# Perceiver block on one core: tile 1's attention moved ahead of tile 0's FFN, Wo split between other work, four buffers for x

## The reference

```python
def fake_quant(x, s, z):
    return (clip(round(x / s + z), 0, 255) - z) * s

x = x + fake_quant(layernorm(x), s1, z1) @ fake_quant(ctx, s2, z2)       # per sequence
qkv = layernorm(x) @ Wqkv          # 32 heads of 32 for q, one head for k and v
p = softmax(causal(q k^T / sqrt(32) + alibi))
x = x + (p v) @ Wo
r = softmax(layernorm(x) @ gate_w.T)                                      # 8 experts
x = x + ((layernorm(x) * (r @ in_scale)) @ sign(weight).T) * (r @ out_scale) + bias
```

## Time and profile before

| | us |
|---|---|
| median of 3 runs | 455.34 |
| lowest, highest | 454.68, 456.38 |
| the profiled execution's own time | 456.7 |
| its span, first to last instruction | 454.9 |
| granted TensorE clock, mean | 0.935 |

### The profile page before, as it was taken

One profiled execution on the slowest core, in us unless ns is written; L12 is line 12 of the kernel. 1 busy time (PEld: TensorE's weight loads), 2 busy tenths in 40 slices (PEclk: granted clock), 3 DMA queues, 4 the chain that ended last, 5 costly groups with the idle time before them and its releaser, 6 DMA issues.

```text
span 454.9 us, 9598 instructions
## 1 busy us (share of the span) xinstructions
PE 382.6 (84%) x3952; PEld 260.4 (57%) x3952; DVE 313.5 (69%) x584; ACT 258.9 (57%) x308; POOL 99.7 (22%) x112
## 2 busy tenths in 40 slices
PE   0446965996699998999899989998999899889665
PEld 0115844964245874587458845884588458745332
DVE  7688576875737859785978597859885965384331
ACT  4687986564875757565756575657665622242110
POOL 4420010004112312231223122312131212021202
PEclk9999975799599999999999999999999999989759
DMA  7999993599876964596459745974491010001001
GB/s 316 378 410 409 406 408 128 186 343 414 242 276 226 324 215 140 170 339 213 138 164 337 220 140 165 330 226 138 156 339 43 0 48 1 4 0 48 0 0 46
DMA packets 30049, 91.97 MB, mean 202 GB/s; under 512 B 8208, under 2 KB 8208, under 8 KB 29968
## 3 DMA queue, kind: packets, MB, share of 16 engines
q1 hardware_dynamic: 27840, 83.40, 51.5%
q10 hardware_dynamic: 2160, 7.87, 4.6%
HBM read 85.50 MB, written 4.19 MB: 197 GB/s over the span
## 4 chain that ended last, share of the span: by engine, by line
PE 68%; DMA 11%; DVE 10%; ACT 5%; issue 4%; SPq 1%; POOL 1%; POOLq 0%; DVEq 0%; ACTq 0%
DMA ring<-ctx 11%; PE R L1408 11%; PE T L1245 8%; PE R L1198 7%; PE R L1200 7%; PE R L1199 7%; PE R L1278 6%; PE R L1280 6%; PE R L1281 6%; PE C L1226 5%; ACT b L475 4%; PE T L1367 4%; DVE Pr L913 2%; DVE XL L1012 1%; PE R L1302 1%
## 5 line engine op out<-in xcount | busy, mean ns | idle before, releaser
L475 ACT ACTIVATE b<-ring,quant,qpar 128x2048 uint8<-128x2048 f32 x64 | 132.9, 2091 | 11.6 <-DMA ring<-ctx 11.5
L1278 PE MATMUL R<-T_hi,Wqkv_hi 128*128 128x128 f16 x512 | 90.9, 223 | 0.0
L1280 PE MATMUL R<-T_lo,Wqkv_hi 128*128 128x128 f16 x512 | 90.8, 223 | 0.0
L1281 PE MATMUL R<-T_hi,Wqkv_lo 128*128 128x128 f16 x512 | 90.7, 223 | 0.0
L1278 PEld LDWEIGHTS R<-T_hi,Wqkv_hi 128*128 128x128 f16 x512 | 51.8, 101 | 0.4
L1408 PE MATMUL R<-sgn,T_hi 128*128 128x512 fp8e4 x128 | 51.7, 404 | 0.0
L1408 PE MATMUL R<-sgn,T_lo 128*128 128x512 fp8e4 x128 | 51.6, 403 | 0.0
L1280 PEld LDWEIGHTS R<-T_lo,Wqkv_hi 128*128 128x128 f16 x512 | 51.2, 100 | 0.2
L1281 PEld LDWEIGHTS R<-T_hi,Wqkv_lo 128*128 128x128 f16 x512 | 51.2, 100 | 0.0
L1226 PE MATMUL C<-b,aT 128*64 128x512 f16 x256 | 39.6, 439 | 13.5 <-ACT b L475 11.3
L1198 PE MATMUL R<-Wo,attT_hi 128*128 128x512 f16 x128 | 48.6, 380 | 0.4 <-DVE attT_lo L944 0.4
(11 more groups left out here) (131 smaller groups left out, 821.8 us busy)
## 6 DMA issues: line engine op xcount, KB each, us to landing
ring<-ctx SPq DMA_DIRECT2D x64, 1024.0 KB, 5.9
ring<-L_attn_Wo SPq DMA_DIRECT2D x4, 1024.0 KB, 7.5
ring<-L_ffn_weight SPq DMA_DIRECT2D x4, 1024.0 KB, 5.7
out<-X ACTq DMA_DIRECT2D x8, 512.0 KB, 2.6
Wo<-L_attn_Wqkv SPq DMA_DIRECT2D x7, 544.0 KB, 15.5
XN<-x ACTq DMA_DIRECT2D x6, 512.0 KB, 3.4
sgn<-L_attn_Wqkv SPq DMA_DIRECT2D x1, 544.0 KB, 17.5
X<-x ACTq DMA_DIRECT2D x1, 512.0 KB, 3.8
```

Source lines behind the costliest of these rows:

```text
L475: e.activation(b8[:, c % BRING, :], ring[:, slot, :], ACT.Identity, scale=qR2, bias=qZ2).then_inc(s_rf[slot], 1)
L1278: e.matmul(dst, hi, rows[0], start=k == 0 and g == 0, stop=False, skip_group_check=True)
L1280: e.matmul(dst, hi, rows[1], start=False, stop=False, skip_group_check=True)
L1281: last = e.matmul(dst, lo, rows[0], start=False, stop=k == KT - 1, skip_group_check=True)
```

## The change

Steps 1 and 2 are woven into one list, `step_1(s, ahead)`, with `ahead = Step(2)`. It issues tile 1's PT, PV, `ta` and projection before tile 0's FFN; tile 0's T2 and router lie between; all of context 2 and the `t1` of tile 2 follow, and then `second_half(2)` goes on at `kv`. Tile 1's queries go to C instead of R2, R3, and tile 0's projection to C too (`project_to`, `query_to`). The T turns are a table (`turns`). The FFN reads its own copies XS, so T16 is free earlier, and there are two vbd pairs. `wo_lo` takes one piece at a time between other work of DVE, `wo_hi` likewise on ACT. `norm0(2)` stands behind tile 1's attention rows and waits for four Ta (both tiles'). SP puts `turn_over(2)` ahead of pieces 4 to 7 of context 2. The scales are loaded behind Wqkv and split on DVE in step 1, with fewer operations. X, XN and X2 become four rotating buffers, summed in place; a load waits for the store of the tile that had the buffer.

```diff
@@ SP
                 if s.is_step(2):
-                    load_context(2, 4, 2)
                     turn_over(2)
-                    load_context(2, 6, 2)
-                else:
-                    load_context(s.i, 4, 4)
-                    if s.i > 2:
-                        turn_over(s.i)
+                load_context(s.i, 4, 4)
+                if s.i > 2:
+                    turn_over(s.i)
                 if s.is_step(0):
                     for k in range(KT):
                         e.dma_start(wqkv_raw[k], wqkv_v[:, k, :]).then_inc(s_lw[k], 16)
+                    e.dma_start(small_sb[:, :], small_in).then_inc(s_const, 16)
+                    for k in range(2):
+                        e.dma_start(scales_raw[k], scales_in[:, k, :]).then_inc(s_scales, 16)
@@ helpers
+        def project_to(m, n):
+            return C[:, 1 - n, :] if m == 0 else R[:, n, :]
+        def query_to(i, n):
+            return C[:, n, :] if i == 1 else R[:, 2 + n, :]
@@ DVE norm0
                 if t > 1:
-                    e.wait_ge(s_Ta, (t - 1) * 2)
+                    e.wait_ge(s_Ta, max((t - 1) * 2, 4))
+                if t == 3:
+                    e.wait_ge(s_T1, 6)
@@ DVE scales
             def scales_by_part():
+                e.wait_ge(s_const, 16)
+                e.wait_ge(s_scales, 32)
+                for k in range(2):
+                    part, raw = scales[:, k, :], scales_raw[k]
+                    link(e.tensor_copy(part, raw))
+                    link(e.tensor_scalar(part, part, sign_sb, None, ALU.mult))
+                    last = e.scalar_tensor_tensor(part, raw, lower_sb, part, ALU.mult, ALU.add)
...
@@ ACT, second part of the new list
+            def step_1(s, ahead):
...
+                wo_hi(3)
+                sign(0)
                 ta_hi(s, 0)
+                q_hi(s, 1)
+                k_hi(s)
+                sign(1)
+                ta_hi(s, 1)
+                q_hi(s, 0)
+                sign(2)
+                sign(3)
+                exp(ahead, 0, 0)
+                exp(ahead, 0, 1)
+                conv(2, 0)
+                pt_hi(ahead, 0, 0)
+                pt_hi(ahead, 0, 1)
+                exp(ahead, 1, 0)
+                exp(ahead, 1, 1)
+                conv(2, 1)
+                pt_hi(ahead, 1, 0)
+                pt_hi(ahead, 1, 1)
+                ta_hi(ahead, 0)
+                t2_copy(s, 0)
+                t2_copy(s, 1)
+                conv(2, 2)
+                router_exp(s)
+                ta_hi(ahead, 1)
+                rt_copy(s)
+                conv(2, 3)
+                xs_hi(s, 0)
+                xs_hi(s, 1)
+                for c in range(4, 8):
+                    conv(2, c)
+                outscale_copy(ahead)
@@ DVE
+            def step_1(s, ahead):
+                softmax_rest(0)
+                scales_by_part()
+                x1(s)
+                pt_lo(s, 0, 0)
+                norm1(s)
+                pt_lo(s, 0, 1)
+                wo_lo(0)
+                t1_lo(s, 0)
+                t1_lo(s, 1)
+                wo_lo(1)
+                attn_rows(s, 0, 0)
+                attn_rows(s, 0, 1)
+                v_lo(s)
+                pt_lo(s, 1, 0)
+                pt_lo(s, 1, 1)
+                wo_lo(2)
+                ta_lo(s, 0)
+                q_lo(s, 1)
+                k_lo(s)
+                attn_rows(s, 1, 0)
+                attn_rows(s, 1, 1)
+                wo_lo(3)
+                ta_lo(s, 1)
+                q_lo(s, 0)
+                stats0(2)
+                softmax_in(1)
+                softmax_rest(1)
+                x2(s, 0)
+                pt_lo(ahead, 0, 0)
+                pt_lo(ahead, 0, 1)
+                x2(s, 1)
+                attn_rows(ahead, 0, 0)
+                norm2(s)
+                attn_rows(ahead, 0, 1)
+                pt_lo(ahead, 1, 0)
+                pt_lo(ahead, 1, 1)
+                ta_lo(ahead, 0)
+                attn_rows(ahead, 1, 0)
+                attn_rows(ahead, 1, 1)
+                norm0(2)
+                router_max(s)
+                router_probs(s)
+                ta_lo(ahead, 1)
+                xs(s, 0)
...
+                x2(ahead, 0)
+                x1(ahead)
+                x2(ahead, 1)
+                norm1(ahead)
+                result(ahead, 0)
+                t1_lo(ahead, 0)
+                t1_lo(ahead, 1)
+                result(ahead, 1)
@@ PE
+            def step_1(s, ahead):
+                context(1, 2)
+                pt(s, 0, 0)
+                pt(s, 0, 1)
+                context(1, 3)
+                t1(s)
+                pv(s, 0, 0)
+                pv(s, 0, 1)
+                kv(s)
+                query(s, 1, low)
+                pt(s, 1, 0)
+                pt(s, 1, 1)
+                query(s, 1, high)
+                ta(s, 0)
+                query(s, 0, low)
+                pv(s, 1, 0)
+                pv(s, 1, 1)
+                tk(s)
+                query(s, 0, high[:2])
+                ta(s, 1)
+                query(s, 0, high[2:])
+                project(s, 0, low)
+                scores(s, 0)
+                scores(s, 1)
+                project(s, 1, low)
+                project(s, 0, high)
+                pt(ahead, 0, 0)
+                pt(ahead, 0, 1)
+                project(s, 1, high)
+                pv(ahead, 0, 0)
+                pv(ahead, 0, 1)
+                pt(ahead, 1, 0)
+                pt(ahead, 1, 1)
+                ta(ahead, 0)
+                t2(s)
+                pv(ahead, 1, 0)
+                pv(ahead, 1, 1)
+                router(s)
+                project(ahead, 0, low)
+                ta(ahead, 1)
+                router_t(s)
+                inscale(s, 0)
+                inscale(s, 1)
+                project(ahead, 1, low)
+                context(2, 0, s)
+                context(2, 1)
+                project(ahead, 0, high)
+                context(2, 2)
+                context(2, 3)
+                project(ahead, 1, high)
+                outscale(ahead, 0)
+                ffn(ahead, 0, low)
+                outscale(ahead, 1)
+                ffn(ahead, 0, high)
+                t1(ahead)
+                ffn(ahead, 1, low)
+                ffn(ahead, 1, high)
```

More of the change, by code:

```diff
@@ L74 @@
 class Step:
[L77 to L92, removed]
     def __init__(self, i):
         self.i = i
-        has = self.stages(i)
-        self.next, self.front, self.middle = has["N"], has["F"], has["M"]
+        self.next, self.front, self.middle = i + 1 < TILES, 0 <= i < TILES, 1 <= i <= TILES
         self.back = i >= 2
-        self.names = [n for r, n in self.order(i) if has[r]]
-        self.used = sum(self.stages(k)[r] for k in range(-1, i) for r, _ in self.order(k))
@@ L103, in is_step, with use @@
     def is_step(self, *steps):
         return self.i in steps
+    def use(self, name):
+        return TURNS[name, self.i - (name not in ("T10", "T11", "Tk")) + 2 * (name == "T0")]
     def bank(self, name):
-        return (self.used + self.names.index(name)) % 2
+        return self.use(name) % 2
     def turn(self, name):
[L111 to L119, removed]
+        return self.use(name) // 2
@@ new lines, in turns, with of @@
+def turns():
+    def of(t, names):
+        return [(n, t) for n in names.split()]
+    uses = of(0, "T0") + of(1, "T0") + of(0, "T10 T11 Tk PT00 PT01")
+    uses += of(1, "T10 T11") + of(0, "PT10 PT11 Ta0") + of(1, "Tk") + of(0, "Ta1")
+    uses += of(1, "PT00 PT01 PT10 PT11 Ta0")
+    uses += of(0, "T20 T21 rl") + of(1, "Ta1") + of(0, "rT is0 is1")
+    for i in range(2, TILES + 1):
+        if i > 2:
+            uses += of(i - 1, "PT00 PT01 PT10 PT11 Ta0 Ta1")
+        uses += of(i, "T10 T11") if i < TILES else []
+        uses += of(i - 1, "T20 T21")
+        uses += of(i, "Tk") if i < TILES else []
+        uses += of(i - 1, "rl rT is0 is1")
+    return {use: n for n, use in enumerate(uses)}
@@ L122 @@
+TURNS = turns()
 class Chain:
@@ L200, in build @@
         kbd = [sb(f"kbd_{p}", [P, 2, 2 * S], F16) for p in ("hi", "lo")]
-        vbd = [sb(f"vbd_{p}", [P, 2, UNITS], F16) for p in ("hi", "lo")]
+        vbd = [[sb(f"vbd{k}_{p}", [P, 2, UNITS], F16) for p in ("hi", "lo")] for k in range(2)]
         Pr = sb("Pr", [P, 2, NH // 2 * S], F32)
@@ L704, in second_half @@
                     load_x(s.i + 1)
-                if m:
+                if m and not s.is_step(2):
                     exp(s, 1, 0)
@@ L1329, in pv @@
                     lhs = [p[:, b, n * P:(n + 1) * P] for p in PT]
[L1330 removed]
+                    last = split_product(dst, lhs, [v[:, b, :] for v in vbd[m % 2]], True, True)
                 last.then_inc(s_pv, 1)
@@ L1407, in ffn @@
                     for part in range(2):
-                        last = e.matmul(R[:, 2 + n, :], T16[part][:, k, :],
+                        last = e.matmul(R[:, 2 + n, :], XS[part][:, k, :],
                                         sgn[:, k, n * HALF:(n + 1) * HALF],
```

(12 more changed lines are left out.)

489 lines of the change are left out of this document (234 added, 255 removed).

## The result

The changed kernel takes 475.76 us (median of 4 runs, 475.36 to 477.68); the kernel before took 455.86 beside it (454.68 to 457.43). The ratio is 1.0443, 95% interval 1.0399 to 1.0487. The forecast was 460.6, range 453.0 to 465.0: the direction was right, and the shift is +19.9 us instead of +5.3, outside the range. The profiled execution took 475.96, its span is 474.2, its mean granted clock 0.909.

The account below looks back on a forecast made before the run. PE was taken to bound tiles 3 to 7. Tile 1's last Ta at 124.7 plus 31.5 us put tile 2's key product at 156.2 against 150.90: 455.34 + 5.3 = 460.6 us, range 453.0 to 465.0.

Parts of the forecast that it names:

- What bounds: Tiles 3 to 7 are bound by PE at 97%; the shift at tile 2's key product is the end's.
- The buffers of x, XS and vbd: In the later periods, they remove waits that cost nothing: price 0, lower bound -1.4 us.
- Start to the key product of tile 1: Up to 77 us: a gain of 2.5 us, tile 1's key product at 77.1 instead of 79.62.
- The scales' steps: On DVE between the last row maximum and x1: 4.6 us, 6.8 at worst; free, or 1.4 late.
- 77 to 113 us: From tile 1's key product into its attention: the 2.5 us gain is used up, the DMA ring runs later.
- Last Ta of tile 1: End of tile 1's attention on PE, with nothing beside it: 124.0 to 125.3 us, taken as 124.7.
- norm0's wait: Tile 2's norm0 waits for all four Ta; PE stands still for 5.6 us after the last.
- The transfer behind it: From the last Ta through norm0, transpose and four loads to context (2,3): 20.6 us, ending after PE's own 18.6.
- What follows it is the same list in both kernels: Behind tile 2's key and value product, the list is unchanged, so the shift there is the end's.
- (c): Dearer rival: clock rises later at 83 to 85.5 and falls in tile 1's attention; +8.3, 463.6 us, chance 0.10.
- (d): Splitting Wo doesn't free the DMA ring, as DVE delays the last piece; in the sum, otherwise 459.2; no chance given.
- Rival (a): Faster: no stalls from 108 to 125 us, last Ta at 117.0, key product 2 at 148.5; 452.9, chance 0.14.

Follow-up runs that it names:

- e0_same: The changed kernel run a second time with nothing edited: 476.63 us, ratio 1.0453 to the kernel before.
- e1_store: The changed kernel with ScalarE's store of tile 0 in step 2 moved behind k_copy and v_copy: 475.49 us, ratio 1.0415.
- e7_wo: The changed kernel with the last Wo piece split right behind the third, ahead of k_lo and the attention rows: 472.28 us, ratio 1.0344.
- e10_late_wo: e9_x3 with the fourth Wo piece split behind tile 0's last attention rows again, as in the changed kernel: 451.97 us, ratio 0.9925.
- e9_x3: e8_best with x(3) loaded before the last context 2 conversions and tile 3's statistics and norm0 right behind tile 2's T1: 452.99 us, ratio 0.9943.
- e8_best: The changed kernel with earlier last Ta and Wo piece, norm0 freed of tok, SP's loads reordered, ScalarE's conversions and store moved: 456.71 us, ratio 1.0011.
- e6_all: The changed kernel with norm0 freed of tok, the last Ta earlier, and ScalarE's store and two context 3 conversions moved: 463.48 us, ratio 1.0165.
- e3_ta: The changed kernel with PE's last Ta issued ahead of the projection's low half: 473.09 us, ratio 1.0406.

## Why the prediction was wrong

**What bounds: half right.** The periods stayed at 45.6 us with 44.17 of PE, and the shift at tile 2's scores is that of the end (19.9 and 19.3 in the two profiled executions). One reading was off without harm: behind slice 5 the DMA line of the earlier trace rows reads 3 and 5, not 0. The buffers of x, XS and vbd brought nothing there, as priced.

**Start to the key product of tile 1: right.** Forecast 77.1, measured 77.69. The scales' steps ended at 68.8 against 68.0 needed, inside the bound.

**77 to 113 us: right, for partly other reasons.** Context (2,0) was converted at 104.27 (forecast 105.6) and the Ta that ended the wait started at 113.05 after 3.31 us idle (114.05 after 3.1). The last Wo piece ended at 93.6 against 95.5. In this execution the clock was at 1.00 from 77.5 us, where I had taken 82.1 (in e0_same from about 81.5); what that gave went into waits that the sum had not, such as 1.43 us ahead of tile 1's PV at 107.70. That the times still came out within some 1 us is in part luck.

**Last Ta of tile 1: 126.35 against 124.7.** Short by 1.65, and the router is the whole of it: 3.56 us against 1.92. The row of 1.92 begins at 111.05, ahead of the 0.50 of the earlier trace rows, in a stretch (110.0 to 112.8) whose clock was 1.00. I put a duration at the full clock into a stretch for which I assumed half of it. The rest of the chain was right.

**norm0's wait: right in kind.** DVE idles 7.53 us until that Ta, PE 6.35 before the rstack transpose (forecast 5.6), no transfer from 113 to 131 and then the four pieces, with those of context 3 right behind. Of the 6.35, 0.74 is one small operation of the router (see the last section).

**The transfer behind it: mis-sized.** From the last Ta to the end of context (2,3) it was 22.6 us against 20.6. The last piece was converted at 145.78, against 143.8 by the forecast moved to the later Ta. By the chain it waited for its slot, until 135.28, since the conversion that frees it stood behind the router on ScalarE; but the third piece, whose slot was free, was 1.4 us late as well, so the slot is not shown to be the reason. And the half projection behind PE's 3.14 us of idling took 4.4 us, not 2.6, as the clock had fallen. The key product came at 161.82 instead of 156.2, and the three make up for it: 1.65 + 2.0 + 1.8 = 5.5 of the 5.6.

**"What follows it is the same list in both kernels": the step that failed.** It is true of PE and not of ScalarE. The prediction wrote down what is queued behind each wait on DVE and SP, and compared only PE's list behind the key product. In the diff `store(0)`, `conv(3, 0)` and `conv(3, 1)` are put between T_hi of tile 2 and `k_copy`; `conv(3, 2)` was already there. Three conversions of 2.10 us each are on record in the earlier trace rows, and the sum on GpSimd ahead of the store could have been placed from the FFN's end. The conversions alone would not have shown it (e1_store); what had to be counted is the store that waits with all three behind it. The sum would have come to 468 or so: 460.6 + 6.1 for the wait and some for the clock behind it (measured 6.07, then half clock from 174.12 to 179.7, which makes 2.8 of lost work; together 8.9 of the 9.0).

**Rivals.** None of them held this. (c), the dearest, ended at 463.6 and dealt with the clock alone. The page of the Trainium skill cited there (TensorE: Matmul & The Clock Gate, oscillation in real kernels) is borne out here more often than the prediction let it be: the clock read 0.59 in 113 to 131 us, 0.77 in 131 to 148, and 0.88 in 148 to 189, each time with waits of 3.1 to 6.4 us between groups of matmuls. It does not hold behind every wait (see the last section). (d) was right on the order of DVE (the load behind the last piece was issued at 93.65 against 93.18), and its price of 1.4 us is left open by e7_wo and e10_late_wo. Rival (a) put the key product at 148.5 if the stalls of 108 to 125 us didn't occur. e9_x3 starts it at 148.29, but not by that way: PE still idles 3.12 us ahead of Ta (113.04), and the last Ta ends at 122.4, where (a) had 117.0. The distance from there to the key product is what shrank, to 25.9 us from the 31.5 of the forecast and the 35.5 measured in the changed kernel. So the new order can have that time, but not with the lists of ScalarE, VectorE and SyncE that the change gave it, and the agreement with (a) is chance.

## What to carry over

When a hand-written order is woven anew, compare the lists of all engines behind the point at which the new order is said to have rejoined the old one, not the list of the bound engine alone. An instruction that starts a transfer and waits for another engine holds up all that is queued behind it: ScalarE stood still for 5.41 us here. A scratch buffer shared by two tiles (tok) turns a reordering into a wait, and an idle buffer in its place was worth 6.5 us here by the medians. A stall of PE is priced at its own length and, where the row shows 0.5 of the clock behind it, at half of the stretch that follows.

## What the hardware showed

A VectorE clip of int16 took 0.43 us at 128.08 in the changed kernel, with GpSimd idle, and 2.46 to 2.47 us at 152.58 (e9_x3) and 153.93 (e8_best), the two values of the earlier trace rows; both long ones start within GpSimd's addition of the bias (2.85 us from 151.90 and 2.86 from 153.25) and end 0.3 us behind it. A far smaller operation shows the same: the router's product over 128x8 took 0.97 us at 131.17 in the changed kernel, within GpSimd's addition of the row sum (1.89 us from 130.22), and 0.23 at 183.58, with GpSimd idle. The float16 product of the scales took 1.15 us beside GpSimd's subtraction (63.32 to 64.73) and 0.47 alone, in the changed kernel:

```profile
63.86 1.15 DVE L864 TENSOR_SCALAR scales<-scales,small_sb 32x1024 f16<-32x1024 f16 x1
...
67.06 0.47 DVE L864 TENSOR_SCALAR scales<-scales,small_sb 32x1024 f16<-32x1024 f16 x1
```

The length of PE's wait alone did not tell whether the clock fell behind it. In e6_all PE idled 2.10 us ahead of 140.34 and ran at 0.50 from 140.8 to 144.0; in e3_ta it idled 2.70 us ahead of 145.82 and stayed at 1.00. PE had been busy for the 4 us ahead of either wait.

The granted clock of one stretch differs between two executions of the same kernel: over 61.6 to 110 us it was 0.89 in the changed kernel's profile and 0.82 in e0_same's, and the scores of tile 2 came 0.66 us apart. The forecast reckoned with one value.
